# Cross attention of the first batch spread over heads 0 to 6, its scaling on GpSimd, and its loads on a second queue

## What is computed

```python
query = einsum('bnc,dc->bnd', ctx, Wq) + bq
key = einsum('bnc,dc->bnd', ctx, Wk) + bk
energy = einsum('bnd,bmd->bnm', query, key)     # 4 x 256 x 256
attention = softmax(energy, axis=-1)
x_m = einsum('bln,bmn->blm', x, attention)      # x: batch x 256 x 256
```

## Time and profile before

| | us |
|---|---|
| median of three runs | 411.34 (411.28 to 411.34) |
| profiled execution | 409.84 |
| its span, first to last instruction | 408.0 |
| PE busy | 388.0 (95%) |
| DVE busy | 284.2 (70%) |
| ACT busy | 266.7 (65%) |
| GpSimd busy | 179.3 (44%) |

### The profile page before, as it was taken

The page is one execution under the profiler, slowest core; times in us unless marked ns, Lnnn a source line. Parts: engine busy times, 40 slices in busy tenths (PEclk is TensorE's granted clock), DMA queues, the critical chain, the costliest instruction groups (busy, mean ns, idle before and its releaser), DMA issues.

```text
span 408.0 us, 8463 instructions
## 1 busy us (share of the span) xinstructions
PE 388.0 (95%) x2559; PEld 346.7 (85%) x2559; DVE 284.2 (70%) x797; ACT 266.7 (65%) x669; POOL 179.3 (44%) x314
## 2 busy tenths in 40 slices
PE   6976999999999999989999989999999999999995
PEld 3666898998888999879999868889989998999994
DVE  2786998886785886877878767477659545744445
ACT  3668997776767685767767677565775744444352
POOL 0243775554664643764463765486956300000000
PEclk9998999999999999999999999999999999999999
DMA  6711421000000000000000099223222222343221
GB/s 200 273 53 53 152 81 28 3 0 2 1 2 27 0 0 0 0 0 0 0 0 0 11 278 332 80 79 93 86 83 85 93 59 78 85 149 100 86 66 51
DMA packets 24677, 28.25 MB, mean 69 GB/s; under 512 B 2961, under 2 KB 17194, under 8 KB 24650
## 3 DMA queue, kind: packets, MB, share of 16 engines
q1 hardware_dynamic: 24650, 27.92, 22.3%
HBM read 26.80 MB, written 1.11 MB: 68 GB/s over the span
## 4 chain that ended last, share of the span: by engine, by line
PE 75%; ACT 9%; DVE 9%; issue 5%; DMA 1%; SPq 1%; ACTq 0%; DVEq 0%
PE bank L704 20%; PE bank L706 20%; PE bank L705 20%; PE bank L834 4%; PE bank L843 3%; PE bank L833 2%; PE bank L806 2%; ACT probs L1089 2%; PE bank L800 1%; ACT probs L1087 1%; ACT swapped L1081 1%; ACT xln L1098 1%; DMA ctx_sb<-in_ctx 1%; PE bank L907 1%; DVE pT_lo L1226 1%
## 5 line engine op out<-in xcount | busy, mean ns | idle before, releaser
L1020 ACT ACTIVATE hid<-bank,b_cols 128x512 f32<-128x512 f32 x48 | 32.9, 686 | 55.6 <-PE bank L706 47.1
L1243 DVE TENSOR_TENSOR hid<-hid,gate_rows 128x512 f32<-128x512 f32 (+1 forms) x44 | 31.9, 724 | 47.7 <-ACT hid L1020 47.5
L1601 POOL TENSOR_SCALAR nprobs<-probs,rsums 128x128 f32<-128x128 f32 x64 | 23.8, 373 | 75.3 <-DVE rsums L1362 66.9
L705 PE MATMUL bank<-w_lo,hid_hi 128*128 128x256 f32 (+1 forms) x200 | 56.3, 282 | 0.0
L1593 POOL TENSOR_TENSOR queryT<-by_cos,by_sin 128x512 f32<-128x512 f32 x32 | 41.1, 1283 | 26.4 <-DVE by_sin L1347 25.4
L1080 ACT COPY swapped<-bank 64x512 f32<-64x512 f32 x40 | 23.3, 583 | 33.1 <-PE bank L706 32.8
L1226 DVE TENSOR_TENSOR hid_lo<-hid,hid_hi 128x512 fp32r<-128x512 f32 x48 | 36.1, 753 | 5.4 <-ACT hid_hi L1041 5.4
L704 PE MATMUL bank<-xT_hi,wq_hi 128*128 128x256 f32 x128 | 38.4, 300 | 1.3 <-issue 1.2
L705 PEld LDWEIGHTS bank<-w_lo,hid_hi 128*128 128x128 f32 (+1 forms) x200 | 37.7, 188 | 2.1
L706 PE MATMUL bank<-x2T_hi,w_lo 128*128 128x512 f32 (+1 forms) x100 | 39.4, 394 | 0.0
L834 PE MATMUL bank<-keyT,queryT 128*128 128x256 f32 x128 | 38.8, 385 | 0.0
(11 more groups left out here) (177 smaller groups left out, 1236.5 us busy)
## 6 DMA issues: line engine op xcount, KB each, us to landing
gate_rows<-gates_d SPq DMA_DIRECT2D x16, 256.0 KB, 3.2
stage<-in_L_attn_q_kernel SPq DMA_DIRECT2D x4, 512.0 KB, 6.6
stage<-in_L_attn_out_kernel SPq DMA_DIRECT2D x4, 512.0 KB, 3.6
w_raw<-in_L_ffn_routed_w SPq DMA_DIRECT2D x2, 1024.0 KB, 9.9
gate_rows<-gates_d SPq DMA_DIRECT2D x8, 224.0 KB, 3.1
gate_rows<-gates_d SPq DMA_DIRECT2D x8, 192.0 KB, 2.8
gate_rows<-gates_d SPq DMA_DIRECT2D x8, 160.0 KB, 2.5
w_raw<-in_L_ffn_routed_w SPq DMA_DIRECT2D x2, 528.0 KB, 7.7
```

Source lines behind the costliest of these rows:

```text
L705: nc.tensor.matmul(o, sh, ml, start=False, stop=False, **kw)
L1020: nc.scalar.activation(hid[:, u % 2, :], z_bank[u % 3][:], ACT.Relu, bias=b1_cols[:, i % NC:i % NC + 1]).then_inc(relu_done, 1)
L1243: nc.vector.tensor_tensor(own, own, gate_rows[rows, i % 3, :], ALU.mult).then_inc(gated, 1)
L1601: nc.gpsimd.tensor_scalar(nprobs[:, u, 0:W], probs[:, u, 0:W], rsums[:, u, 0:1], 1.0, ALU.mult, ALU.mult)
```

## The change

Order. "ctx turned" stays behind x0 and x1 on PE, but "ctx projected" goes behind k0. Energies 0 and 1 go behind score 0, attT 0 behind score 2, attT 1 behind k1, energies 2 and 3 behind turn 0, attT 2 behind turn 2, attT 3 behind v1, and small turned behind turn 3. On ACT and DVE the pieces q0 and k come before the context's copies, and piece q1 before slot q0.

The new order of PE is: x0, x1, ctx turned, q0, k0, ctx projected, q1, q2, score 0, energy 0 and 1, score 1, q3, score 2, attT 0, k1, attT 1, score 3, turn 0, energy 2 and 3, score 4, turn 1, q4, score 5, turn 2, attT 2, v1, attT 3, score 6, turn 3, small turned, v0, score 7 and on as before. Of ACT from slot q2: exp 0, e_exp 0 and 1, slot q3, exp 1, piece q2, attT 0, slot k1, exp 2, attT 1, probs_hi 0, piece v, e_exp 2, exp 3, probs_hi 1, e_exp 3, slot q4, exp 4, probs_hi 2, piece q3, slot v1, attT 2, exp 5, attT 3, probs_hi 3, slot v0. Of DVE from slot q2: top 0, e_top 0, top 1, e_top 1, recip 0, e_rsum 0, top 2, slot q3, recip 1, e_rsum 1, piece q2, top 3, slot k1, recip 2, probs_lo 0, piece v, e_top 2 and 3, top 4, recip 3, probs_lo 1, e_rsum 2 and 3. Of GpSimd: q0, k0, q1, q2, normalise 0, e_norm 0, normalise 1, q3, e_norm 1, normalise 2, k1, normalise 3, e_norm 2 and 3, normalise 4, q4.

Banks: energies 2 and 3 use banks 6 and 7 too, behind attT 0 and 1 on ACT; turn 0 no longer waits for attT 3, and the first `values` waits for attT 2 on ACT. The two scalings of e_norm are GpSimd's, with a semaphore e_normed; DVE keeps the reciprocal. The context's five loads are issued by ACT ahead of its other work, the context first; SP issues the identity before x. One of three keep_busy products is gone.

```diff
@@ -115,18 +115,15 @@
 PIECE_NAMES = ["q0", "k", "q1", "q2", "v", "q3", "o0", "o1", "o2", "o3"]
-PIECE_AT = dict(zip(PIECE_NAMES, (-2.1, -2.05, -0.9, 2.2, 3.1, 5.4, 6.6, 8.1, 10.1, 12.1)))
+PIECE_AT = dict(zip(PIECE_NAMES, (-2.4, -2.35, -1.5, 2.2, 3.1, 5.4, 6.6, 8.1, 10.1, 12.1)))
 ONCE_AT = {
-    "pe": {"ctx turned": -2.4, "ctx projected": -2, "energy 0": -0.9, "energy 1": -0.85,
-           "energy 2": 0.2, "energy 3": 0.25, "attT 0": 1.1, "attT 1": 1.15, "attT 2": 2.1,
-           "attT 3": 2.15, "small turned": 4.1},
-    "act": {"ctx turned": -2.35, "ctx projected": -2, "e_exp 0": -0.3, "e_exp 1": -0.25,
-            "e_exp 2": 0.8, "e_exp 3": 0.85, "attT 0": 1.3, "attT 1": 1.35, "attT 2": 2.5,
-            "attT 3": 2.55, "small turned": 4.3},
-    "dve": {"ctx turned": -2.35, "ctx projected": -1.95, "e_top 0": -0.7, "e_top 1": -0.65,
-            "e_top 2": 0.3, "e_top 3": 0.35, "e_norm 0": -0.1, "e_norm 1": -0.05, "e_norm 2": 1.7,
-            "e_norm 3": 1.75},
-    "pool": {},
+    "pe": {"ctx turned": -2.3, "ctx projected": -0.9, "energy 0": 0.3, "energy 1": 0.35, "attT 0": 2.3,
+           "attT 1": 2.8, "energy 2": 3.3, "energy 3": 3.35, "attT 2": 5.3, "attT 3": 5.8, "small turned": 6.3},
+    "act": {"ctx turned": -2.2, "ctx projected": -0.85, "e_exp 0": 0.9, "e_exp 1": 1.4, "attT 0": 2.5,
+            "attT 1": 2.9, "e_exp 2": 3.7, "e_exp 3": 4.0, "attT 2": 5.5, "attT 3": 5.9, "small turned": 6.5},
+    "dve": {"ctx turned": -2.2, "ctx projected": -0.85, "e_top 0": 0.45, "e_top 1": 0.6, "e_rsum 0": 1.3,
+            "e_rsum 1": 1.8, "e_top 2": 3.4, "e_top 3": 3.45, "e_rsum 2": 4.0, "e_rsum 3": 4.35},
+    "pool": {"e_norm 0": 1.35, "e_norm 1": 1.85, "e_norm 2": 4.05, "e_norm 3": 4.4},
 }
@@ -470,7 +467,7 @@
         y_done, twice_done, y_tile_done = sem("y_done"), sem("twice_done"), sem("y_tile_done")
         final, std_done, x3_by_act, x3_by_dve = sem("final"), sem("std_done"), sem("x3_by_act"), sem("x3_by_dve")
         stored = sem("stored")
-        idle_set = sem("idle_set")
+        idle_set, e_normed = sem("idle_set"), sem("e_normed")
         dve_passed, pool_passed, act_passed = sem("dve_passed"), sem("pool_passed"), sem("act_passed")
@@ -553,7 +550,7 @@
             return prob_bank[1] if is_last(b, g, blk) else pv_bank
-        E_BANK = [6, 7, 4, 5]
+        E_BANK = [6, 7, 6, 7]
         idle_rows = nprobs[:].rearrange("p a k -> p (a k)")
@@ -583,13 +580,8 @@
                              r_b[first:first + mid * P].rearrange("(n p) -> n p", p=P)).then_inc(ld_small, 16)
                 sp.dma_start(b1_rows[NC - 1:NC, 0:LAST], row(r_b[first + mid * P:NR * FF])).then_inc(ld_small, 16)
+            sp.dma_start(ident[:], ident_c).then_inc(ld_ident, 16)
             sp.dma_start(xb[:], x[0].rearrange("(t p) c -> p t c", p=P)).then_inc(ld_xb, 16)
-            sp.dma_start(ident[:], ident_c).then_inc(ld_ident, 16)
-            sp.dma_start(xw[:, 0, :], xwq).then_inc(ld_ctx, 16)
-            sp.dma_start(xw[:, 1, :], xwk).then_inc(ld_ctx, 16)
-            sp.dma_start(xb_cols[:, 0:1], xbq.rearrange("(d a) -> d a", a=1)).then_inc(ld_ctx, 16)
-            sp.dma_start(xb_cols[:, 1:2], xbk.rearrange("(d a) -> d a", a=1)).then_inc(ld_ctx, 16)
-            sp.dma_start(ctx_sb[:], ctx_v).then_inc(ld_ctx, 16)
             for n in range(4):
                 sp.dma_start(stage_view(n), PIECES[n][0]).then_inc(ld_stage[n % 4], 16)
                 if n == 1:
@@ -835,8 +827,6 @@
                                  start=True, stop=True).then_inc(scored, 1)
             def turn(b, h):
-                if isinstance(b, int) and b == 0 and h == 0:
-                    after("act", "attT 3")
                 e.wait_ge(norm_done, head_count(b, h))
                 e.wait_ge(pT_done, head_count(b, h - 2))
                 for k in range(3):
@@ -848,6 +838,8 @@
                 e.wait_ge(pT_done, head_count(b, G * g + G - 1))
                 e.wait_ge(emptied, slot_count(b, LAST_V))
+                if isinstance(b, int) and b == 0 and g == 0 and blk == 0:
+                    after("act", "attT 2")
                 if not is_last(b, g, blk):
                     e.wait_ge(oT_done, pv_count(b, g, blk) - 1)
                 f = slice(g * D, (g + 1) * D)
@@ -910,6 +902,8 @@
                 elif work[:-2] == "energy":
                     c = int(work[-1])
                     after("act", "xqT 1"), after("dve", "xkT 1")
+                    if c >= 2:
+                        after("act", f"attT {c - 2}")
                     for t in range(TT):
                         r = slice(c * T + t * P, c * T + (t + 1) * P)
                         mm = nc.tensor.matmul(bank[E_BANK[c]][:, t * T:(t + 1) * T], xqT[:, r],
@@ -927,7 +921,7 @@
                 else:
                     c = int(work[-1])
-                    after("dve", f"e_norm {c}")
+                    e.wait_ge(e_normed, c + 1)
                     for k in range(KC):
                         for t in range(TT):
                             mm = nc.tensor.transpose(bank[E_BANK[c]][:, k * T + t * P:k * T + (t + 1) * P],
@@ -938,7 +932,7 @@
                      "values0": lambda b, g: values(b, g, 0), "values1": lambda b, g: values(b, g, 1),
                      "out0": lambda b, g: project_out(b, g, 0), "out1": lambda b, g: project_out(b, g, 1)}
             e.wait_ge(idle_set, 1)
-            keep_busy(2)
+            keep_busy(1)
             e.wait_ge(ld_ident, 16)
             take_turn("pe", 0, (0, "once"), doers)
             with e.Fori(1, B) as b:
@@ -1157,6 +1151,11 @@
             doers = {"slot": slot, "exp": softmax_exp, "probs_hi": probs_hi, "once": once,
                      "heads_hi0": lambda b, g: heads_hi(b, g, 0), "heads_hi1": lambda b, g: heads_hi(b, g, 1),
                      "normed 1": lambda b, _: normed(b, 0), "normed 2": lambda b, _: normed(b, 1)}
+            e.dma_start(ctx_sb[:], ctx_v).then_inc(ld_ctx, 16)
+            e.dma_start(xw[:, 0, :], xwq).then_inc(ld_ctx, 16)
+            e.dma_start(xw[:, 1, :], xwk).then_inc(ld_ctx, 16)
+            e.dma_start(xb_cols[:, 0:1], xbq.rearrange("(d a) -> d a", a=1)).then_inc(ld_ctx, 16)
+            e.dma_start(xb_cols[:, 1:2], xbk.rearrange("(d a) -> d a", a=1)).then_inc(ld_ctx, 16)
             take_turn("act", 0, (0, "once"), doers)
             with e.Fori(1, B) as b:
                 take_turn("act", b, (0, 1), doers)
@@ -1417,10 +1416,6 @@
             def after_act(name):
                 e.wait_ge(act, place("act", name))
-            def settle():
-
-                e.wait_ge(dve, n[0])
-
             def once(work, of):
                 if work == "piece":
                     piece(of)
@@ -1440,12 +1435,7 @@
                 else:
                     c = int(work[-1])
                     after_act(f"e_exp {c}")
-                    step(nc.vector.reciprocal(e_rsum[:, c, :], e_sum[:, c, :]), f"e_rsum {c}")
-                    settle()
-                    for t in range(TT):
-                        ins = nc.vector.tensor_scalar(e_exp[:, c, t, :], e_exp[:, c, t, :], e_rsum[:, c, t:t + 1], None,
-                                                      ALU.mult)
-                    step(ins, work)
+                    step(nc.vector.reciprocal(e_rsum[:, c, :], e_sum[:, c, :]), work)
             for s in (score_read, rsum_done, pT_done):
                 e.sem_inc(s, AHEAD)
@@ -1646,11 +1636,19 @@
                     settled(nc.gpsimd.tensor_tensor(newton[:], newton[:], by_root(factor[:], 3), ALU.mult))
                 assert done[0] == NEWTON_STEPS
+            def once(work, of):
+                c = int(work[-1])
+                e.wait_ge(dve, place("dve", f"e_rsum {c}"))
+                for t in range(TT):
+                    ins = nc.gpsimd.tensor_scalar(e_exp[:, c, t, :], e_exp[:, c, t, :], e_rsum[:, c, t:t + 1], 1.0,
+                                                  ALU.mult, ALU.mult)
+                ins.then_inc(e_normed, 1)
+
             for s in (norm_done, turned):
                 e.sem_inc(s, AHEAD)
-            doers = {"slot": slot, "normalise": normalise, "keep": keep, "norm 1": lambda b, _: layer_norm(b, 0),
+            doers = {"slot": slot, "normalise": normalise, "keep": keep, "once": once, "norm 1": lambda b, _: layer_norm(b, 0),
                      "norm 2": lambda b, _: layer_norm(b, 1)}
-            take_turn("pool", 0, (0,), doers)
+            take_turn("pool", 0, (0, "once"), doers)
             with e.Fori(1, B) as b:
                 take_turn("pool", b, (0, 1), doers)
@@ -1685,8 +1683,7 @@
                             "small turned": ["smallT"]}),
     "act": once_order("act", {"ctx turned": ["xwT", "ctxT 0"], "ctx projected": ["xqT 0", "xqT 1"],
                               "small turned": ["smallT"]}),
-    "dve": ["b1 cleared"] + once_order("dve", {"ctx turned": ["ctxT 1"], "ctx projected": ["xkT 0", "xkT 1"],
-                              **{f"e_norm {b}": [f"e_rsum {b}", f"e_norm {b}"] for b in range(B)}}),
```

(1 more changed line is left out.)

## The result

The changed kernel takes 418.37 us (median of four, 417.64 to 418.44) against 411.34 for the kernel before measured beside it: ratio 1.0168, 95% interval 1.0154 to 1.0181. The forecast was 413.8 with a range up to 416.5: the sign is right, the size is not. The profiled execution took 418.39 us, its span 416.6, with a mean granted clock of 0.985 (0.996 before).

A forecast was written before the change was run, and what follows sets the result against it. PE was taken to set the pace from the second batch, so the start of slot v0 decides: +1.7 us chain, +1.1 clock, -0.3 after v0 gave +2.5, 413.8 us on the median of 411.34, range up to 416.5.

The forecast's parts named there:

- T: Start of slot v0 on PE, 45.07 us before the change; the chain put it at 46.8, before the clock's cost.
- S: Start of slot q0 on PE, taken as 10.6 us, between 9.9 and 14.0.
- Steps 1 to 8: Chain across PE, ACT, DVE and GpSimd from S to T: 35.65 us plus ten handovers of 0.05, so S + 36.2.
- Step 4: GpSimd: q3's rope sum, 1.27 us, waits out a scaling stretched beside DVE's piece, then e_norm 1, 0.95: 2.2 us.
- Step 5: PE: attT 1 waits for e_norm 1, with score 3 behind it; 0.44 and 0.65, together 1.1 us.
- Step 6: DVE waits in top 3 for score 3, with k1, piece v and e_top 2 behind: 4.05 us.
- steps 7 and 8: ACT runs dense from e_exp 2 to attT 3, 8.8 us; then PE's small turned waits for attT 3, 0.25.
- The clock: PE falls to 1.2 GHz behind its longer waits, at least once; 1.1 us on the chain, between 0 and 2.1.
- X: When batch 1's x is turned and batch 1 starts, 67.01 us before the change; expected near 69.5.
- The late context: Rival: ACT's queue finishes only with piece q1, S is 13.4 to 14.0; +4.5 us, 415.8; chance 0.14.
- The faster case: Rival: GpSimd's scalings end before PE needs them, ACT bounds from exp 0, T 42.2; -2.9 us, 408.5; chance 0.18.
- The wash: Rival: S at 9.9, no clock fall on the chain, 0.8 us taken up after v0; 411.5 us; chance 0.18.

The follow-up runs named there:

- e2: Changed kernel with the two bias loads on a semaphore of their own, awaited only where the biases are added: 415.23 us, ratio 1.0083.
- e7: Changed kernel with three keep_busy products at the start instead of one and four ahead of ctx turned instead of one: 417.09 us, ratio 1.0123.
- e9: Changed kernel with both the biases' own semaphore and the extra keep_busy products (three, and four ahead of ctx turned): 417.12 us, ratio 1.0128.
- e13: Changed kernel with the biases' own semaphore and extra keep_busy products, but two instead of four ahead of ctx turned: 414.42 us, ratio 1.0084.
- e12: Changed kernel with PE kept busy by unread products in its waits ahead of attT 0 and attT 1: 416.73 us, ratio 1.0119.
- e14: Changed kernel with biases apart, filled start (two products ahead of ctx turned), scaling on DVE, attT 1 to 3 and small turned later: 409.11 us, ratio 0.9942.
- e4: Changed kernel with the eight e_exp scalings back on DVE, right behind their reciprocals: 414.91 us, ratio 1.0090.
- e6: Kernel before the change with only the e_exp scaling moved to GpSimd: 413.35 us, ratio 1.0056.
- e10: Changed kernel with biases apart, filled start (four products ahead of ctx turned), attT 1 to 3 and small turned later, scaling on GpSimd: 411.41 us, ratio 1.0005.

## Why the prediction missed, step by step

T was late by 4.95 us (52.85 against 47.9, which is 46.8 with the 1.1 for the clock): 3.4 us at the start, where S = 10.6 and the 0 for keep_busy failed, and 1.6 in the sizes of the chain behind it.

**The loads and S: wrong, the first big miss.** ACT started on piece q0 at 7.97 us (8.0 predicted) and DVE's split ended at 10.27 (8.0 + 1.08 + 1.22 is 10.3; the text has 10.4). What failed is the sentence that took S as 10.6: one semaphore counts all five loads, and the last is the second bias, issued at 3.22 behind two pieces that SP had already issued. It landed at 10.9 instead of 5.6, while the context itself was there by 5.9. The text had the mechanism as its upper bound (the four small loads finishing late) and set it aside by taking a value near the lower end. The landing of the last of the five was the row to take. The transposes could start only at 10.97 instead of 9.45: 1.5 us.

**keep_busy at nothing: wrong.** The cover named, the loads, hides the time of a product, not what it does to the clock. Before, these products had PE at the full level by 5.09 us; after, the transposes and what follows them up to slot q0 took 2.05 us instead of 1.15 and slot q0 2.39 instead of 1.45: 1.8 us. At k0 both terms together are 3.4 us: 15.41 against 12.05 (10.6 and a slot of 1.45). Of the time, e2 gives back 3.1 us, e7 1.3, and e9 and e13 show that these overlap.

**Steps 1 to 8: right in mechanism and order, 1.6 us short in sizes.** From k0 to T the prediction had 34.75 us, 35.85 with the clock, and the trace has 37.44. Up to attT 1 it was 0.8 us short; 0.5 of this is by_sin of slot q2 on DVE, which took 1.15 us instead of 0.68 beside the sum of q1 on GpSimd (25.16 us). Step 4, the price of GpSimd, is exact: 1.52 for the stretched scaling, then 1.26 and 0.93. Step 5 had 1.1 us from attT 1 to top 3; e12 shows 1.5 at full level, so 0.4 was missing, and the other 1.1 of the 2.6 is the clock. Step 6 had 4.1 with its handover and took 4.2; steps 7 and 8 had 9.15 and took 9.4; step 8 was released by ACT as said.

**The clock: right in kind and price, not in length.** One or two falls of the length of the earlier trace rows, 3.4 us, were expected, worth 1.1; one of 10.24 us came. Its price on the chain was still 1.1 us, by the comparison with e12 above, since only attT 1 and score 3 are on the chain while it lasts: energies 2 and 3, which took 3.32 us at half clock, were done before DVE came to them.

**After v0: right.** 0.2 us were taken up, 0.3 predicted.

**From X to the end: not foreseen.** It took 343.8 us in the profile after and 342.8 before. Batches 1 and 2 account for 0.3 of it; that the rest lies in the clock's fall at the very end (4.29 us long instead of 2.22) is argued, not tested. And the profiled execution before was 1.5 us under its median, the one after is at its median: profiles differ by 8.6 us, medians by 7.0. Against the profiles the forecast of +2.5 was off by 6.1 us, against the medians by 4.6: the smaller miss is luck.

**The rivals.** The late context named the right place and nearly the right time of the first slot product (13.4; it was 13.02), but partly by luck: it had ACT's queue finish at 12.8, and the last bias landed at 10.9. The clock at the start, which it lacked, made up the rest, and slowed slot q0 as well, so its 415.8 is too low. The faster case hung on attT 1 being ready at about 29 us; it was 36.6. In e14, with k0 at 12.18, attT 1 starts at 30.0 and T is 41.56, close to its 42.2, but this does not bear out its reckoning: ACT stands idle there for 1.9 us ahead of e_exp 2, and small turned is no longer ahead of v0. The wash needed S at 9.9 and no fall; neither came.

**The engine for the scaling.** The Trainium skill (GPSIMD Engine Reference, "4.1 Engine selection") has GpSimd at about line rate for one-input work. The rows agree for the operation: 0.93 for a pair against 1.09 on DVE. e4, e6 and e10 show losses of 3.5, 1.5 and 1.35 us all the same, by what stands ahead of it in the queue and beside it on DVE, with the clock's falls in the sum.

## What to carry to other kernels

When loads move to a second queue, look at which landing ends each shared wait: the last issue of the small ones counts, not the big ones, and what is needed later can have a semaphore of its own. An instruction that fills PE's idle time isn't free to remove, and isn't free to add once the loads are there. Before a step is moved to an emptier engine, read what stands ahead of it in that engine's queue; and after one wait is cured, look for the next one that takes it up.

## What was unexpected of the hardware

- The granted clock fell near most of PE's longer waits, not all: in the changed kernel for 10.24 us with waits of 2.30 and 3.25 us near, in the kernel before near one of 1.90. In e12 it held through the same waits filled with products and fell at the next. But in e4 a wait of 2.19 us up to 42.98, and in e7 one of 2.74 up to 45.57, had no fall until 49.55 and 51.26. In e4, e7 and e9 a fall right behind v0 kept 1.5 us of the gain in T from reaching X.
- Two loads of 0.5 KB in 4-byte pieces landed 2.2 and 2.4 us after issue in the kernel before, 7.0 and 7.7 when they were issued behind others on the second queue, and with them first on that queue the rate fell to 27 GB/s for 1.2 us and a load of 512 KB took 9.9 us instead of 4.9.
